# Reordering the hand-over from weight splitting to the first expert tiles, with two weight steps moved from TensorE to VectorE

## What is computed

```python
x = x + attn(layernorm(x))            # q, k: relu(proj), 32 heads of 64; out = q (k^T v) / (q . sum k), then @ Wo + bo
xf = layernorm(x)                      # 2048 x 512
scores = xf @ gate_w.T + gate_b + bias # 8 experts
top_scores, top_idx = top_k(scores, 2)
gates = softmax(top_scores)
h = silu(einsum('td,ehd->teh', xf, w1) + b1)      # w1: 8 x 352 x 512
y = einsum('teh,edh->ted', h, w2) + b2            # w2: 8 x 512 x 352
x = x + sum over the two chosen experts of gate * y
```

## Time and profile before

| | |
|---|---|
| median of three runs | 1009.13 us (1009.12 to 1009.3) |
| the profiled execution, whole | 1010.6 us |
| its span, first to last instruction | 1008.9 us |
| granted TensorE clock over the span | 1.000 |

### The profile page before, as it was taken

The page is one execution under the profiler, slowest core; times in us unless marked ns, Lnnn a source line. Parts: engine busy times, 40 slices in busy tenths (PEclk is TensorE's granted clock), DMA queues, the critical chain, the costliest instruction groups (busy, mean ns, idle before and its releaser), DMA issues.

```text
span 1008.9 us, 17463 instructions
## 1 busy us (share of the span) xinstructions
PE 995.8 (99%) x5019; PEld 839.2 (83%) x5020; DVE 688.1 (68%) x1554; ACT 513.2 (51%) x1322; POOL 255.7 (25%) x413
## 2 busy tenths in 40 slices
PE   8999999999999999999999999999999989999998
PEld 7888888888888888888788888888888879989996
DVE  6888655665666677767878778887888764544544
ACT  5444444444444447755556555555554954343442
POOL 1000000000000002222433232333333555555554
PEclk9999999999999999999999999999999999999999
DMA  7002501000000012343211121111125645555653
GB/s 263 13 30 84 209 22 40 23 21 21 21 22 21 21 63 63 105 172 116 44 44 51 42 52 42 42 42 42 42 66 149 203 123 102 107 102 101 107 108 48
DMA packets 46862, 75.35 MB, mean 75 GB/s; under 512 B 6090, under 2 KB 18555, under 8 KB 46691
## 3 DMA queue, kind: packets, MB, share of 16 engines
q1 hardware_dynamic: 37010, 56.04, 18.3%
q0 software_dynamic: 9808, 18.79, 10.2%
HBM read 53.14 MB, written 23.50 MB: 76 GB/s over the span
## 4 chain that ended last, share of the span: by engine, by line
PE 93%; DVE 3%; ACT 1%; DMA 1%; issue 1%; SPq 0%; POOL 0%; POOLq 0%; DVEq 0%; ACTq 0%
PE pK L1627 16%; PE pK L1629 16%; PE pK L1628 16%; PE pA L1627 6%; PE pA L1629 6%; PE pA L1628 6%; PE pX L1627 6%; PE pX L1629 5%; PE pX L1628 5%; PE pA L1761 3%; PE pT L1970 2%; PE pT L1707 2%; PE pX L1988 1%; PE pA L1895 1%; PE pK L1895 1%; DMA xn<-in_attn_hidden_states 1%
## 5 line engine op out<-in xcount | busy, mean ns | idle before, releaser
L973 ACT ACTIVATE qs<-q,nrec 128x64 f32<-128x64 f32 x512 | 129.6, 336 | 88.1 <-DVE nrec L1357 85.7
L594 POOL TENSOR_TENSOR wv_lo<-wv_in,wv_hi 128x512 fp32r<-128x512 f32 x4 | 5.2, 1296 | 403.5 <-ACT wo_hi L894 403.5
L1627 PE MATMUL pA<-k_hi,xn_hi 128*128 128x512 f32 x256 | 100.9, 394 | 0.6 <-DVE k_lo L1232 0.6
L1627 PE MATMUL pK<-wk_hi,xnT_hi 128*128 128x512 f32 (+1 forms) x256 | 100.1, 391 | 0.4 <-DVE wk_lo L1212 0.3
L1627 PE MATMUL pK<-wq_hi,xnT_hi 128*128 128x512 f32 x256 | 100.4, 392 | 0.0
L1629 PE MATMUL pK<-wq_hi,xnT_lo 128*128 128x512 f32 x256 | 99.9, 390 | 0.0
L1629 PE MATMUL pA<-k_hi,xn_lo 128*128 128x512 f32 x256 | 99.8, 390 | 0.0
L1628 PE MATMUL pK<-wk_lo,xnT_hi 128*128 128x512 f32 (+1 forms) x256 | 99.7, 390 | 0.0
L1628 PE MATMUL pA<-k_lo,xn_hi 128*128 128x512 f32 x256 | 99.7, 389 | 0.0
L1629 PE MATMUL pK<-wk_hi,xnT_lo 128*128 128x512 f32 (+1 forms) x256 | 99.7, 389 | 0.0
L1628 PE MATMUL pK<-wq_lo,xnT_hi 128*128 128x512 f32 x256 | 99.7, 389 | 0.0
(11 more groups left out here) (291 smaller groups left out, 2446.8 us busy)
## 6 DMA issues: line engine op xcount, KB each, us to landing
w_in<-in_ffn_w SPq DMA_DIRECT2D x22, 256.0 KB, 4.2
w_in<-in_ffn_w SPq DMA_DIRECT2D x8, 704.0 KB, 5.8
xn<-in_attn_hidden_states SPq DMA_DIRECT2D x16, 256.0 KB, 6.2
wv_in<-in_attn_Wv SPq DMA_DIRECT2D x16, 256.0 KB, 2.8
wo_in<-in_attn_Wo SPq DMA_DIRECT2D x16, 256.0 KB, 3.0
wk_in<-in_attn_Wq SPq DMA_DIRECT2D x4, 1024.0 KB, 5.7
xnT_dram<-xnT SPq DMA_DIRECT2D x4, 1024.0 KB, 11.5
x_in<-in_attn_hidden_states SPq DMA_DIRECT2D x16, 256.0 KB, 2.7
```

What stands on the lines that cost most here:

```text
L973: i = nc.scalar.activation(qs[:, s], q[:, s], ACT.Copy, scale=nrec[:, b * HC + h:b * HC + h + 1])
L1627: nc.tensor.matmul(dst, lhs[0], rhs[0], start=start, stop=False)
```

## The change

Six edits, in one stretch of the kernel:

1. Steps 22 and 31 leave `PE_STEPS`: VectorE subtracts them instead.
2. On GpSimd, the comparison of tile numbers with `up_to` (two instructions) is put in front of the wait for the scatters and of the read of `meta_in`.
3. On GpSimd, `gather(0)` and `gather(1)` are put in front of `put_b2(6)` and `put_b2(7)`.
4. On VectorE, `META_AT` goes from 32 to 34, so the steps 31, 32 and 33 are subtracted in front of the copies to `slot_token` and `far`; a wait for `w_put` 34 and for eight TensorE subtractions stands ahead of step 32.
5. On ScalarE, `act_gT(2)` goes between `act_h(0)` and `act_h(1)`, and the wait for `hT_ones` behind them. On TensorE, `pe_gT(2)` goes in front of `pe_hT(0)`.
6. On VectorE, `dve_gT(1)` goes in front of `hT_fill`.

```diff
-        PE_STEPS = [*range(4), 11, 15, 19, 22, 25, 31, 37]
+        PE_STEPS = [*range(4), 11, 15, 19, 25, 37]
@@ GpSimd
             tab(pool.tensor_scalar(meta_row[:, :].unsqueeze(1), row8[:, :, 0:1], float(MROWS - 1), None, ALU.min))
+            tab(pool.tensor_tensor(by8(cmp[:, :]), wide(iota_j[:, :], E), many(up_to, TW), ALU.subtract))
+            tab(pool.tensor_scalar(by8(cmp[:, :]), by8(cmp[:, :]), 0.0, None, ALU.is_ge))
             for b in range(2):
                 pool.wait_ge(s_meta[b], 16 * NT)
             pool.indirect_dma_start(meta_in[:, :], None, meta_rows, bass.IndirectOffsetOnAxis(meta_row[:, :].bitcast(U32), 0)
                                     ).then_inc(s_metain, 16)
-            tab(pool.tensor_tensor(by8(cmp[:, :]), wide(iota_j[:, :], E), many(up_to, TW), ALU.subtract))
-            tab(pool.tensor_scalar(by8(cmp[:, :]), by8(cmp[:, :]), 0.0, None, ALU.is_ge))
             fold(by8(cmp[:, :]), E)
...
+            gather(0)
+            gather(1)
             put_b2(6)
             put_b2(7)
-            gather(0)
-            gather(1)
             gather(2)
@@ ScalarE
-            act.wait_ge(hT_ones, 2)
             act_h(0)
-            act_h(1)
             act_gT(2)
+            act_h(1)
+            act.wait_ge(hT_ones, 2)
             act_silu(0, first_expert)
@@ VectorE
-            META_AT = 32
+            META_AT = 34
...
-            lo_steps(11, META_AT)
+            lo_steps(11, 32)
+            dve.wait_ge(w_put, 34)
+            dve.wait_ge(w_sub_put, sum(k < 32 for k in PE_STEPS))
+            lo_steps(32, META_AT)
             dve.wait_ge(meta_put, 1)
...
+            dve_gT(1)
             hT_fill()
-            dve_gT(1)
             put_gates()
@@ TensorE
             pe_h(1, expert(1))
-            pe_hT(0)
             pe_gT(2, 0)
+            pe_hT(0)
             pe.wait_ge(w_lo_ready, len(DVE_STEPS))
             pe_hT(1)
```

More of the change, by code:

```diff
@@ L1169, in _ @@
             first_expert = act.value_load(tile_expert[0:1, 0:1], min_val=0, max_val=E - 1)
+            act_h(0)
+            act_gT(2)
+            act_h(1)
             act.wait_ge(hT_ones, 2)
-            act_h(0)
-            act_h(1)
-            act_gT(2)
             act_silu(0, first_expert)
@@ L2016, in _ @@
             pe_h(1, expert(1))
+            pe_gT(2, 0)
             pe_hT(0)
-            pe_gT(2, 0)
             pe.wait_ge(w_lo_ready, len(DVE_STEPS))
```

## The result

The changed kernel is slower, by a little: 1010.72 us (1009.88 to 1012.84) against 1009.35 us, 22 runs of each side by side, a ratio of 1.0015 with a 95% interval of 1.0009 to 1.0021. That is +1.4 us with +0.9 to +2.1 around it, where -0.15 was forecast. The profiled execution of the changed kernel has a span of 1009.8 us and a time of 1011.6.

What follows compares the result with a forecast made beforehand. It took the read of `meta_in` and the two loads behind it to bound tile 0's start; 0 (edit 1) + 0 (edit 4) + 0.43 (edit 2) + 0 (edit 3) - 0.58 (edits 5, 6) = -0.15, giving 1009.0 us, range 1008.3 to 1010.1.

Steps and rivals of the forecast that it cites:

- the gathers' effect on the second load: DMA queues ahead of step 43: earlier gathers take no bandwidth from the last expert load, 0 us.
- edits 5 and 6: Tiles 0 to 2: tile 2's matmuls start 6.28 us after tile 0's in place of 6.86, a gain of 0.58.
- the delay of the read: GpSimd: the comparison put ahead makes the read of `meta_in` start later, delaying loads and tile 0, +0.43 us.
- What bounds the kernel, and edit 1: Ahead of tile 0: the `meta_in` read and two loads set the date, so TensorE's saved 1.46 us become waiting, worth 0.
- I take no clock effect: TensorE around 800 to 1000 us: clock 1.00 in all three stretches despite idling, so no clock change was counted.
- Edit 4: VectorE: the later META_AT covers the added subtractions, and the copy still finds VectorE free, worth 0.
- third rival: Gathers take bandwidth from the second load: step 43 later by 0.65 to 1.3 us, sum +0.5 to +1.15, chance 0.17.
- The rule on turn-taking: DMA engines alternate between queue rows packet by packet, so an earlier gather would interleave with and delay the last load.
- The sum: All edits together: 0 + 0 + 0.43 + 0 - 0.58 = -0.15 us, median 1009.0.
- The range: Measured time: 1008.3 to 1010.1 us, meant to leave out no more than two in ten.

Runs made afterwards that it cites:

- second comparison: The unchanged changed kernel (all six edits) timed again against the kernel before: 1010.82 us, ratio 1.0006 (0.9997 to 1.0015).
- only5_timed: The kernel before with edit 5 alone, timed: 1011.40 us, ratio 1.0013 (1.0004 to 1.0022).
- undo23: The changed kernel with edits 2 and 3 undone: 1010.24 us, ratio 0.9998 (0.9989 to 1.0007) to the kernel before.
- load6_gap: The kernel before with edit 6 and expert 6's load issued already behind step 24's transposes: 1010.53 us, ratio 1.0006 (0.9997 to 1.0015).
- load6_early: The kernel before with edits 1, 2, 4, 6 and expert 6's load issued once the scatters landed: 1010.99 us, ratio 1.0010 (1.0001 to 1.0019).

## Why the prediction was wrong, step by step

Two steps failed: the gathers' effect on the second load was put at 0 (it is 0.45 us on the mean and 0.82 in the profile of the changed kernel), and edits 5 and 6 at -0.58 (they are 0 to +0.1 together). A third, the delay of the read, was put too high, which partly hid the other two.

- **What bounds the kernel, and edit 1**: right. Steps 34 and 35 moved up, TensorE idled ahead of `meta_transpose` (1.27 us; the forecast of about 2 had the read later than it came), and the freed 1.46 us were gone. The step "I take no clock effect" was wrong in kind: kernels with edit 1 have dips (3 in 33 executions of those without edit 5). What they cost there isn't settled.
- **Edit 4**: right, worth nothing.
- **Edit 2, the read**: mis-sized. The price of +0.43 came from the gap of 0.50 ahead of the fourth gather; behind the comparison the gap was 0.29. With edit 2 the read starts 2.46 behind `meta_row` (2.45 in two) in the seven profiles of the table that have it; without it, it followed the scatters' landing, 2.26 in before and 1.52 to 2.68 elsewhere. So it costs 0.1 to 0.2 on average, and the loads weren't later in the changed kernel.
- **Edit 3 with edit 2, the gathers**: the step that failed. "So I take 0" rested on 24 packets of q0 against 519 in a kernel in which the gathers came 1.6 us behind the load. The gather's advance was underrated too, by two terms: the read wasn't delayed, and the issue follows `ids_ready` by 0.27, not 0.50. It came 1.1 earlier relative to the load, where the forecast's dates (0.3 earlier, load 0.43 later) made it 0.7. The third rival was right in kind: step 43 at 814.10 with packets in between. Its price of 0.65 to 1.3 lay at the upper side of what the profiles show (0.2 to 0.85, mean 0.45) and beyond it.
- **The rule on turn-taking** (the Trainium skill, "DMA: Bandwidth & Descriptors", Queues, rings and completion order) told the direction. But this trace has most of the load's packets moved ahead of the gathers' and only the last 14 between them, and the loss was smaller than the rival had it.
- **Edits 5 and 6**: wrong in sign for the pair. Edit 6 gave 0.4 (forecast 2.31 - 2.05 = 0.26). For edit 5, `pe_hT(1)` came on its forecast date, but the forecast let tile 2 start 0.2 behind its end. The term left out is what the loop's entry needs behind `pe_hT(1)`: 1.18 to 1.35 us from its start in every profile. Of this, 0.70 is "issue" in the changed kernel; whether it goes into reading the expert's number, the branch or something else, no run tells. So tile 2 became due at 5.66 + 1.21 = 6.87, not 6.28. The profile of before had the figure: these transposes start at 821.55 there and tile 2 at 822.89, 1.34 behind.
- **The sum**: with the sizes measured, in the order edits 1, 4, 2, 3, 6, 5, 0 + 0 + 0.1 + 0.45 - 0.4 + 0.5 = +0.65, near the 0.76 of the profiles and inside the second comparison's interval, but under the first's, which begins at 0.9. Up to 0.6 us of the first comparison isn't located. Dips don't account for it: the two of its executions with a mean clock of 0.997 took 1010.69 and 1010.76, and the slowest, 1012.84, had 0.999. Even T0, which no edit can move, lies between 772.9 and 774.4 in these profiles.
- **The range** ended at 1010.1, the result is 1010.7. Of the difference, 0.2 is the base: the forecast started from the kernel before at 1009.13 (three runs), beside the changed kernel it had 1009.35. The third rival added to a lost edit 5 would have reached it; the cases were priced one at a time, as if all but one term stayed at its forecast.

## What to carry to other kernels

Before work is taken off the busiest engine, follow what it waits for next: here a table read and two loads, so 1.46 us less work was 1.3 us more waiting. An engine off the path that gets ahead issues its transfers earlier, and the question is which transfer on the path they then run beside. When instructions are swapped in a hand-written order ahead of a loop, date the loop's first instruction from the last one in front of it, by the distance that the profile shows, and not only from its data.

## What the runs showed of the hardware

- A slightly longer wait of TensorE is paid twice in some executions. Behind 1.65 us of idling in two pieces around `pe_hT(1)`, the granted clock went from 1.00 to 0.50 for 3.4 us in both profiles of edit 5 alone, and in `only5_timed` cost 1.55 us where TensorE sets the pace; three more of the 11 executions of `only5_timed` have the same mean clock of 0.997. In the other profiles with a dip it lies behind one wait for the read of `meta_in`, of 1.76 (`undo23`), 1.77 (`load6_gap`) and 3.12 us (`load6_early`). The kernel before idles 0.25 and 0.82 around `pe_hT(1)` and showed none. What sets it off in one execution and not the next stays open.
- Packets of a queue fed by software, coming while a large load is still queued, mostly waited for it, but the load's last packets were then served among them (14 of the load's among 124 of theirs in the changed kernel, 1 among 136 before). How late the load's user starts varied by 0.6 us between two profiles of the same kernel (6.71 and 6.13).
- A load issued into a gap of idle DMA engines isn't free for a small read behind it: issued 27.9 or 26.2 us behind T0, 3.9 us or less ahead of the read's own issue near 30, 704 KB delayed the use of the table by 1.7 and 1.9 us.
